# One raw-weight room and two activation rooms in a fused four-layer kernel, with a new instruction order ahead of its tile loop

## The reference, cut to what matters

```python
x = x + tanh(g_xattn[0]) * smoothquant_experts(layernorm(x), fside, ctx)     # layer 1, x is (4, 512, 512)
x = x + tanh(g_ffn[0])   * bit_linear_ffn(layernorm(x), gate_w, val_w, out_w) # layer 2, hidden 2048
x = x + tanh(g_xattn[1]) * (layernorm(x) @ softmax(q @ k.T))                  # layer 3, q, k from ctx
x = x + tanh(g_ffn[1])   * top2_moe(layernorm(x), router_w, down_w, up_w)     # layer 4
# smoothquant linear, per batch b (z=0: x with fside; z=1: silu(gate)*up with ctx)
s  = sqrt(max|x| over rows / max|w| over rows)       # needs column maxima of BOTH operands
xq = round(x/s / row scale); wq = round(w*s / row scale)
y  = xq @ wq.T * scales
```

## Time and profile before

| what | us |
|---|---|
| three timed runs | 467.65, 470.37, 471.56; median 470.37 |
| the profiled execution's own time | 470.85 |
| its span in the trace | 469.1 |
| PE busy in the span | 420.2 (90%) |
| DVE busy | 379.7 (81%) |
| ACT busy | 350.4 (75%) |
| POOL busy | 220.7 (47%) |
| mean granted PE clock | 0.981 of full |

### The profile page before, as it was taken

One profiled execution on the slowest core, in us unless ns is written; L12 is line 12 of the kernel. 1 busy time (PEld: TensorE's weight loads), 2 busy tenths in 40 slices (PEclk: granted clock), 3 DMA queues, 4 the chain that ended last, 5 costly groups with the idle time before them and its releaser, 6 DMA issues.

```text
span 469.1 us, 7365 instructions
## 1 busy us (share of the span) xinstructions
PE 420.2 (90%) x2183; PEld 246.0 (52%) x2183; DVE 379.7 (81%) x955; ACT 350.4 (75%) x574; POOL 220.7 (47%) x343
## 2 busy tenths in 40 slices
PE   4876879977978988689999999999999999999986
PEld 3766647635646434245455545545545554554563
DVE  3889597998893788587898898889889899888853
ACT  1399877796898998857787787778788788777532
POOL 3292684588796744365343333333424333341220
PEclk9987979999999999999999999999999999999999
DMA  8999597354459301511221331231224123122101
GB/s 303 388 386 280 131 340 110 129 168 80 143 131 228 88 7 33 103 30 26 47 47 45 68 59 43 62 75 37 54 68 46 45 67 63 43 67 67 45 25 45
DMA packets 84936, 49.53 MB, mean 106 GB/s; under 512 B 70936, under 2 KB 73496, under 8 KB 83872
## 3 DMA queue, kind: packets, MB, share of 16 engines
q1 hardware_dynamic: 84896, 49.06, 40.3%
HBM read 28.33 MB, written 4.19 MB: 69 GB/s over the span
## 4 chain that ended last, share of the span: by engine, by line
PE 62%; DVE 10%; ACT 9%; DMA 7%; issue 6%; POOL 3%; SPq 2%; ACTq 0%; POOLq 0%; DVEq 0%
PE p_out L1892 11%; PE p_gate L1797 11%; PE p_out L1804 11%; PE p_val L1797 10%; PE p_tr L1779 3%; PE p_out L1826 3%; PE p_out L1852 3%; DMA att_t<-in_L_ffn_gate_w 2%; DMA ctx_sb<-in_ctx 2%; ACT q_room L1282 2%; DMA att_t<-in_L_ffn_out_w 2%; DVE h_max L772 1%; DVE rowmax L812 1%; PE p_val L1748 1%; ACT gate_t L1265 1%
## 5 line engine op out<-in xcount | busy, mean ns | idle before, releaser
L1797 PE MATMUL p_val<-val_t,q_room 128*128 128x512 fp8e4 x256 | 65.7, 379 | 1.4 <-ACT p_val L1407 1.4
L1797 PE MATMUL p_gate<-gate_t,q_room 128*128 128x512 fp8e4 x256 | 65.7, 379 | 0.7 <-DMA q_room<-q_room 0.6
L1804 PE MATMUL p_out<-att_t,qT_room 128*128 128x512 f32 x120 | 55.4, 603 | 1.4 <-ACT qT_room L1227 1.4
L1892 PE MATMUL p_out<-out_t,ws_f 128*128 128x512 fp8e4 x240 | 54.5, 379 | 1.4 <-DMA ws_f<-ws_f 1.4
L594 POOL TENSOR_TENSOR rstd<-mv,ln_eps 128x1 f32<-128x1 f32 x48 | 9.1, 189 | 95.0 <-DVE mv L863 87.9
L1397 ACT ACTIVATE p_gate<-w_slots,seed_scale 128x512 f32<-128x512 f32 x64 | 43.4, 682 | 10.2 <-POOL seed_scale L615 8.9
L892 DVE TENSOR_TENSOR act_f<-p_val,ctx_sb 128x512 f32<-128x512 f32 x64 | 44.1, 689 | 8.4 <-PE p_val L1797 6.1
L1382 ACT ACTIVATE ctx_sb<-p_gate,bcol 128x512 f32<-128x512 f32 x64 | 43.6, 682 | 8.0 <-issue 4.1
L894 DVE TENSOR_REDUCE mu<-act_f 128x1 f32<-128x512 f32 x64 | 43.9, 686 | 2.2
L1407 ACT ACTIVATE p_val<-w_in,seed_scale 128x512 f32<-128x512 f32 x64 | 43.3, 679 | 0.6 <-DVE act_f L892 0.6
L621 POOL TENSOR_TENSOR x_all<-x_all,q_room 128x512 f32<-128x512 f32 x16 | 20.5, 1281 | 45.7 <-ACT q_room L1325 39.1
(11 more groups left out here) (243 smaller groups left out, 989.9 us busy)
## 6 DMA issues: line engine op xcount, KB each, us to landing
att_t<-in_L_ffn_out_w SPq DMA_DIRECT2D x6, 1024.0 KB, 5.0
w_in<-in_fside_BxS2xS SPq DMA_DIRECT2D x4, 1024.0 KB, 7.6
att_t<-in_L_ffn_gate_w SPq DMA_DIRECT2D x4, 1024.0 KB, 13.1
att_t<-in_L_ffn_val_w SPq DMA_DIRECT2D x4, 1024.0 KB, 11.7
out_dram<-x_all SPq DMA_DIRECT2D x15, 256.0 KB, 2.3
x_all<-in_x SPq DMA_DIRECT2D x2, 1024.0 KB, 10.0
x_all<-in_x SPq DMA_DIRECT2D x1, 2048.0 KB, 18.2
ctx_sb<-in_ctx SPq DMA_DIRECT2D x4, 512.0 KB, 5.9
```

The source lines that it names most:

```text
L1797: last = nc.tensor.matmul(bank[:, c % 2, :], x_t[n % 2][:, k * P:(k + 1) * P], w_t[m][:, k, cols], start=False, stop=k == KD - 1, skip_gro ...
L1804: last = nc.tensor.matmul(p_out[:, 0, :], lt_c[:, k * P:(k + 1) * P], att_t[:, bass.ds((n // T) * (KD * S) + k * S, S)], start=k == 0, sto ...
L1892: last = nc.tensor.matmul(p_out[:, 0, :], p_t[:, k * P:(k + 1) * P], w_t[2][:, k, :], start=k == 0, stop=k == KH - 1)
```

## The change

The two buffers of `w_in` become one, and `act_f` becomes two. `fside_load(b)` now waits for `scaled_weights(0, b-1)`; `h_normalise(b)` for the rounding of batch b-2's activations. All five engines get another order ahead of the tiles. No computing instruction is added or removed: the helper calls are the same, each once.

```diff
-        act_f = sb("act_f", [P, T * D], F32)
+        act_f = [sb(f"act_f{r}", [P, T * D], F32) for r in range(2)]
-        w_in = [sb(f"w_in{r}", [P, T * D], F32) for r in range(2)]
+        w_in = sb("w_in", [P, T * D], F32)
-        bias_gate, bias_val = w_slots[...], w_in[0]
-        u = act_f
+        bias_gate, bias_val = w_slots[...], w_in
+        u = act_f[0]
+        def act_of(z, b):
+            return act_f[b % 2] if z == 0 else a_f
         def wt_of(z, b):
-            return w_in[b % 2] if z == 0 else ctx_sb[b % 2]
+            return w_in if z == 0 else ctx_sb[b % 2]
                 def fside_load(b):
-                    need(sp, a_ws[0], b - 1)
+                    need(sp, a_ws[0], b)
                 def val_b_load():
-                    sp.wait_ge(a_ws[0], NB - 1)
+                    sp.wait_ge(a_ws[0], NB)
                 def h_normalise(b):
-                    need(pool, a_q16[0], T * (2 * b - 1))
+                    need(pool, a_q16[0], T * (2 * b - 3))
                 def columns(z, b, r, k):     # PE
-                            pe.wait_ge(fside_loaded[b % 2], 16 * (b // 2 + 1))
+                            pe.wait_ge(fside_loaded, 16 * (b + 1))
```

SP's order, from the x loads on (the calls not shown keep their place):

```diff
+                x_load(2, slice(2, NB))
                 x_load(1, 1)
-                x_load(2, slice(2, NB))
-                fside_load(1)
-                val_load(1)
                 val_load(0)
                 val_load(2)
+                val_load(1)
                 val_load(3)
+                fside_load(1)
                 small_loads()
+                integers(0, 0, 0)
                 integers(0, 0, 1)
-                integers(0, 0, 0)
+                out_load(1)
+                ctx_load(0)
+                ctx_load(1)
                 out_load(0)
                 fside_load(2)
-                ctx_load(0)
-                out_load(1)
-                fside_load(3)
                 integers(0, 1, 0)
                 integers(0, 1, 1)
                 out_load_next(2)
-                ctx_load(1)
+                out_load_next(3)
                 integers(1, 0, 0)
                 integers(1, 0, 1)
-                out_load_next(3)
+                fside_load(3)
                 ctx_load(2)
...
                 integers(1, 1, 0)
+                integers(1, 1, 1)
                 out_load_again(0)
-                val_b_load()
-                integers(1, 1, 1)
-                integers(0, 3, 0)
+                ctx_load(3)
                 out_load_again(1)
+                integers(0, 3, 0)
                 integers(0, 3, 1)
-                ctx_load(3)
+                out_b_load()
                 gate_b_load()
+                val_b_load()
+                x_transpose(0)
                 integers(1, 2, 0)
                 integers(1, 2, 1)
-                x_transpose(0)
                 x_transpose(1)
                 x_transpose(2)
-                out_b_load()
```

More of the change, by code:

```diff
@@ L257, in flamingo_gated_kernel @@
         x_loaded = [sem(f"x_loaded{n}") for n in range(3)]
-        fside_loaded = [sem(f"fside_loaded{r}") for r in range(2)]
+        fside_loaded = sem("fside_loaded")
         ctx_loaded = [sem(f"ctx_loaded{r}") for r in range(2)]
@@ L345, in fside_load @@
                 def fside_load(b):
-                    need(sp, a_ws[0], b - 1)
-                    sp.dma_start(tiles(w_in[b % 2][:, :]), fside[bass.ds(b, 1)].rearrange("b (t p) d -> p (b t) d", p=P)).then_inc(fside_loaded[b % 2], 16)
+                    need(sp, a_ws[0], b)
+                    sp.dma_start(tiles(w_in[:, :]), fside[bass.ds(b, 1)].rearrange("b (t p) d -> p (b t) d", p=P)).then_inc(fside_loaded, 16)
                 def ctx_load(b):
@@ L1068, in _ @@
                 h_scaled_act(1)
-                w_sum(2, 0)
                 h_dequantise(0, 2)
@@ L1085, in _ @@
                 t_reciprocal(0, 0)
-                h_statistics(3)
+                w_sum(2, 0)
                 column_max(0, 2, 0, 0)
@@ L1443, in _ @@
                 w_round(2)
+                w_transposed(0)
                 smooth_rows(0, 0)
-                w_transposed(0)
+                rounded(0, 0, 0)
                 w_transposed(1)
                 w_transposed(2)
+                w_sum(1, 1)
+                w_sum(1, 3)
                 w_transposed(3)
-                rounded(0, 0, 0)
-                w_sum(1, 1)
                 rounded(0, 0, 1)
-                w_sum(1, 3)
                 small_weights()
@@ L1496, in _ @@
                 t_transposed(1, 1)
+                smooth_rows(1, 1)
+                t_exponential(1, 2)
                 rounded(0, 2, 1)
-                t_exponential(1, 2)
                 t_exponential(1, 3)
-                smooth_rows(1, 1)
+                scale_row(0, 2)
                 w_sum(2, 3)
@@ L1563, in _ @@
                 gate_seed(1, 1)
-                q_norm(2)
+                b_gate(1, 0)
+                val_seed(1, 1)
+                q_scaled(2)
+                b_gate(1, 1)
+                gate_seed(1, 2)
+                gate_seed(1, 3)
+                val_seed(1, 2)
+                rounded(1, 3, 0)
+                rounded(1, 3, 1)
+                b_gate(1, 2)
+                silu_loaded()
+                t_transposed(3, 0)
                 t_transposed(3, 1)
                 b_scaled(0, 2)
-                b_gate(1, 0)
-                q_scaled(2)
-                gate_seed(1, 2)
-                b_gate(1, 1)
-                rounded(1, 3, 0)
-                gate_seed(1, 3)
-                rounded(1, 3, 1)
                 b_scaled(0, 3)
-                val_seed(1, 2)
+                scale_row(1, 3)
                 val_seed(1, 3)
-                scale_row(1, 3)
                 t_exponential(3, 2)
                 t_exponential(3, 3)
-                b_gate(1, 2)
+                gate_seed(2, 0)
                 b_gate(1, 3)
+                gate_seed(2, 1)
                 t_transposed(3, 2)
@@ L1921, in _ @@
                 columns(0, 0, 1, 3)
+                clock_raised(2)
                 columns(0, 0, 0, 0)
@@ L1936, in _ @@
                 w_transpose(3)
+                clock_raised(7)
+                clock_raised(6)
+                clock_raised(5)
+                w_total(1)
+                clock_raised(4)
                 columns(0, 1, 1, 0)
+                scale_row(0, 0)
                 columns(0, 1, 1, 1)
                 columns(0, 1, 1, 2)
-                scale_row(0, 0)
-                clock_raised(5)
                 columns(0, 1, 1, 3)
+                small_weights()
                 columns(0, 1, 0, 0)
+                w_transpose(4)
                 columns(0, 1, 0, 1)
-                w_total(1)
                 columns(0, 1, 0, 2)
-                small_weights()
-                w_transpose(4)
                 columns(0, 1, 0, 3)
                 w_transpose(5)
-                clock_raised(4)
                 products(0, 0, 0)
@@ L1997, in _ @@
                 columns(1, 1, 0, 0)
+                columns(1, 1, 0, 1)
+                columns(0, 3, 1, 0)
+                columns(0, 3, 1, 1)
                 t_transpose(1, 0)
                 t_transpose(1, 1)
-                columns(1, 1, 0, 1)
                 t_energies(1, 2)
+                rows(1, 1)
                 t_energies(1, 3)
-                rows(1, 1)
+                scale_row(0, 2)
                 columns(0, 3, 1, 2)
```

294 lines of the change are left out of this document (142 added, 152 removed).

## The result

Over 22 runs each, the kernel after took 468.28 us (median, 466.83 to 472.13) and the kernel before 471.15 (467.65 to 474.01): a ratio of 0.9944, 95% interval 0.9928 to 0.9960. That is 2.9 us or 0.6%, a real gain and a small one. The forecast was 467.4.

The account below looks back on a forecast made before the run. PE bounds the unchanged tile loop, so time won ahead of it passes one for one; DVE, then ACT, bound stretches there. Terms +2.3 - 1.0 - 0.5 - 2.6 - 1.2 = -3.0 us gave 467.4 us, range 462.5 to 474.5.

Parts of the forecast that it names:

- The early part, forecast +2.3: 20 to 56 us: the single raw-weight room makes `smooth(0, 1)` end at 57.9 instead of 55.6, +2.3 us.
- held by fillers and not by the DMA: Before batch 1's columns: `columns(0, 1, 1, 0)` starts at 46 us, behind clock fillers, three of them taking 5.7 us.
- Nothing is lost in bandwidth: Early loads: fside(1) lands at 42 to 43 us, but the val chunks come earlier by as much.
- The second activation room, forecast 0: Early part: it hides nothing that was on the path; taken as 0, its worth between 0 and 1 us.
- 56 to 73, forecast -1.0 and no wait for `w_in`: Batch 0 to 1: 1.0 us regained, `t_query_key(0)` 1.3 later; fside(2) lands at 73.1, 0.8 us before PE wants it.
- The first rival, full clock: Early part and `t_query_key(0)`: clock stays at its upper level, another 4.3 us gained, 463.1 us; chance 0.21.
- 73 to 117, forecast -0.5: DVE's stretch: `h_statistics(3)` leaves, -2.8, and `w_sum(2, 0)` comes in, +2.28; net -0.5 us, standing +0.8.
- 117 to 165, forecast -2.6: ACT's stretch: ready calls fill its idle places and the reload is earlier, -2.0; `scale_row(1, 2)` moves, -0.6 us.
- 165 to 209, forecast -1.2: Path to `b_output(0)`: `smooth_rows(1, 3)` and SP's list release `integers(1, 3, *)` sooner, -1.2 us, bounds 0 and -3.
- tanh, forecast 0: `tanh_gates`, moved to a stretch with Exp's table, needs no table load: 0, with 2.6 us kept for the range.
- The second (raw weights on the path): Late fside(2) landing stops PE at `columns(0, 2, 1, 0)`: +3.3 us in all, 473.7 us; chance 0.24.
- The third (cancel): Whole kernel: early loss and late gain cancel, 470.4 us; chance 0.13.

Follow-up runs that it names:

- run 5: `round_first`: the kernel after with `rounded(0, 3, 0)` ahead of `w_transposed(9)` on ACT; 468.15 us, ratio 0.9950 to the kernel before.
- run 6: The kernel after without the clock fillers `clock_raised` 7, 6, 5 and 4; 467.35 us, ratio 0.9927 to the kernel before.
- run 7: The kernel after with SP issuing `p_transpose(0, 0)` and `(0, 1)` ahead of `integers(1, 3, *)`; 468.04 us, ratio 0.9921 to the kernel before.
- run 8: The kernel after with the changes of run 6 and run 7 joined; 469.16 us, ratio 0.9948 to the kernel before.
- run 9: The kernel after with before's rooms, `h_normalise(2)` and the fside loads placed as those rooms want, loads early; 470.88 us, ratio 0.9999 to before.
- run 10: The kernel after with before's rooms, `h_normalise(2)` behind `h_hidden(0, 3)`, fside(1) behind the value weights; 469.02 us, ratio 0.9945 to before.
- run 12: Run 11 with `h_reciprocal_deviation(2)` ahead of `w_round(4)` and `h_statistics(3)` ahead of `column_max(0, 1, 0, 3)`; 466.76 us, ratio 0.9918 to before.
- run 11: Before's rooms and before's order on all engines up to `smooth(0, 1)`, then the change's order; 474.28 us, ratio 1.0070 to the kernel before.
- run 4: The kernel after with `out_load_again(1)` put back between `integers(0, 3, 0)` and `integers(0, 3, 1)` on SP; 474.45 us, ratio 1.0095 to before.
- the third column: Table column for the profiled execution of run 5, which has the order of the kernel after up to 130 us; span 463.8 us.
- start_fixed: The kernel of run 12: before's start mended, then the change's later order; 466.76 us, ratio 0.9918 to the kernel before.
- run 3: The kernel before with SP's list from `integers(1, 1, 1)` on as in the change, except `x_transpose(0)`; 471.33 us, ratio 0.9995 to before.
- run 1: The kernel before with the change's rooms, only the fside loads and val's bias load moved on SP; 483.86 us, ratio 1.0269 to before.

## Why the prediction came out right, step by step

The total was 0.9 us off, and its sign and size rest on the whole sum; several terms were off in ways that offset each other, and that the sum still came so close is in part luck.

The profiles, one execution of each kernel, can be cut in two at the first context maximum. From there to the end of the span before takes 395.8 us, and the kernel after 393.5. Runs 5, 6, 7, 8, 9, 10 and 12, which have the new order from there on, take 392.5, 392.7, 392.3, 393.2, 393.5, 394.0 and 393.4 (run 11, whose DVE had stood still just ahead of that point, 395.1; run 4, with its stall, 399.0). So the later part is worth 1.8 to 3.5 us, where the forecast had 4.3 (0.5, 2.6 and 1.2). Up to that maximum the same kernels take anything from 69.7 to 76.8 us, against 73.3 before, where the forecast had 1.3 later. The median's -2.9 is thus about what the later part alone gives: its forecast was too large, and the forecast early loss, which would have to be taken off it, isn't seen in the median.

**The early part, forecast +2.3: late, but by something else.** In the profile it is +4.1, in the third column +1.5 (56.97 against 55.46). The start of the columns was right within half a microsecond (46 forecast, 45.52 measured), the landing of fside(1) late by two (42 to 43 forecast, 44.9 measured). The failing step is "held by fillers and not by the DMA": I gave three fillers 5.7 us at the lower clock, and they took 3.41 us, most of it at the upper level (0.78 in the mean from 38 to 40 us, 1.00 from 40 on) and inside a wait (the row at 37.81). `w_total(1)` holds the columns, with the DMA level with it (run 6); that the forecast time was right is luck. I had overlooked that moving `w_total(1)` ahead of the columns ties them to the landing of the last value chunks. "Nothing is lost in bandwidth" says nothing of what PE has waiting for those chunks.

The excess of 1.8 us arose behind that start. From the first column to the last reciprocal the kernel after takes 14.0 us; the forecast had 11.9 to the end of `smooth(0, 1)`. DVE waited 1.16 and 1.87 us for PE (the rows at 46.44 and 49.00), where `scale_row(0, 0)` took 1.92 us at the lower level (the row at 46.19) and stands between the first two columns. In the third column, at the upper level, the same stretch takes 12.85 us (44.12 to 56.97). That price of the clock isn't in the forecast's sum.

**The second activation room, forecast 0.** Right as far as run 10 goes: it puts both rooms back at once, and their sum is nothing measurable. It doesn't show each by itself.

**56 to 73, forecast -1.0 and no wait for `w_in`.** No engine waited for fside(2), issued at 68.73 and landed 6.3 us later. The stretch gave back more, 2.5 us of its 4.1. In the kernel before, `smooth(0, 1)` didn't set the pace here: PE stood for `ctx_load(0)`, which the chain that ended last shows too (first row PE's timeline, second row the chain):

```profile
64.42 1.40 PE L1741 MATMUL p_val<-ident,ctx_sb 128*128 128x128 f32 x8 [2.25 <-DMA ctx_sb<-in_ctx]
```

```profile
55.84 8.54 DMA ctx_sb<-in_ctx
```

In the kernel after it waits for ACT instead (the row at 67.25), 2.8 us later and not 4.1. `t_query_key(0)` then began 2.55 us later, not 1.3, and ran at the lower level again, but for 5.40 us against 6.35. At the upper level it takes 3.70 us: so it ran in the profiles of runs 5, 6 and 7 and of `start_fixed`. In those of runs 8, 9 and 10 it took over 6 us. The first rival, full clock, therefore happens in some executions and not in others; in runs 5 and 7 the order up to this call is that of the kernel after, unchanged. Standing at the end of the stretch: +1.6 measured, +1.3 forecast.

**73 to 117, forecast -0.5.** At `row_scales(0, 2, 0)` the kernel after is 0.45 behind, where I expected 0.8 at the end of the stretch. From the first context maximum to there it gave 1.14 us, in the third column just as much (22.06 us in both, 23.20 before).

**117 to 165, forecast -2.6.** The largest term, and too large. `products(0, 3, 0)` starts at 149.56 against 149.63. So the packing gave 0.5 us from 97 on, not 2.0: ACT is indeed fuller by 0.9 us in the second window, but `rounded(0, 3, 0)` comes 2.7 and `rounded(0, 3, 1)` 5.5 us later than before, as the text had it "against". And ACT isn't what ends this stretch. The chain that ended last goes, in before, from the late reload over POOL to `w_transpose(11)`:

```profile
138.91 7.26 DMA att_t<-in_L_ffn_out_w
...
148.73 1.07 PE p_val L1656 x16
```

In the kernel after it stays on POOL from 124.57 until 145.83, but for gaps of at most 0.6 us each:

```profile
124.57 1.12 POOL w_slots L529
...
129.59 4.93 POOL ws_f L562 x4
...
138.15 2.49 POOL x_all L591 x2
...
144.70 1.13 POOL w_slots L529
145.88 1.07 PE p_val L1659 x16
```

So the change took the reload off the path (run 4 puts it back), and POOL's own list, which the forecast had not looked at, stands there next. That also fits run 5, where another order on ACT moved nothing in the total. No run here changes POOL's list, so this is read from the chain and not tested.

Behind `products(0, 3, 0)` the first `b_chunk` is 1.7 us sooner (164.02), which looks like the forecast's -1.8, and isn't: the change puts it ahead of a 1.03 us product, and at `columns(1, 3, 0, *)` the two kernels are level, 170.72 and 170.85. The reload's mechanism was right; taken out of the new order it costs 6 us (run 4), put into before's order it gains nothing in the total (run 3).

**165 to 209, forecast -1.2.** Measured -0.6. `smooth_rows(1, 3)` is 1.4 us sooner (178.26), but `integers(1, 3, *)` start only 0.3 sooner: `rounded(1, 3, 0)`, at 185.23 against 185.56, now stands behind two gate seeds and a value seed. The wait for `p_transpose` stays, 1.52 us. The cause is as forecast, half of the size is gone.

**tanh, forecast 0.** It runs in 0.20 us at 83.17, between works of Exp and with the next table load only at 87.81. That fits the table sets as the Trainium skill gives them ("ScalarE: Activation LUTs", section "Table sets: the hidden batching unit"). The load itself takes 1.28 us, and the next function starts at 89.11, 1.30 us after the load began. The Trainium skill (same page, section "What ACT_TABLE_LOAD costs") counts 2.66 us with a drain, which this trace doesn't show.

Sum: of the -3.0 forecast, the profiled executions show -0.7 and the medians -2.9. The profile of after fell in a long execution. Against the run with its order up to 130 us and the clock high, the same path is 4.7 us shorter at `c_attend(0)`. So the median's agreement isn't the sum of the profile's terms; what the early terms are worth in a typical execution, between the two columns, stays open to about 2 us. Of the signs named, the loop's period, the missing table load and the missing wait for `w_in` came; `smooth(0, 1)` was 1.6 us later than the 58 named, DVE idle near 70 was 2.25 us and not 3 to 6, and the first loop step 0.51 us sooner and not 3.

**The rivals.** The second (raw weights on the path) didn't come true with the new order: no engine waits for `w_in` in the profile after. With the rooms alone it does, in a kernel 2.7% slower (run 1). The third (cancel) is excluded by the interval. The rooms named in the title give nothing measurable: the order gives the gain, and the single raw-weight room needs that order.

## What to carry to other kernels

When storage and order change together, time the new order with the old storage before crediting the storage: here the new order alone gave the 0.6%, and the rooms nothing that could be measured. A hand-written list for one engine can't be judged or moved alone: one load placed ahead of transposes cost 18 us of queue in one kernel, and was needed in another. A point that comes late is a loss only where it is on the chain: `smooth(0, 1)` was 4.1 us late and the next joint, the first context maximum, 1.6, since before had waited there for a load. And before an engine's list is called the bound, look whether the chain runs over it: from 125 to 146 us it ran over POOL, although ACT was the fuller of the two (19.49 us of 20 against 12.98 from 140 to 160).

## What the runs showed of the hardware

Two executions with the same instructions in the same order up to 130 us stood 2.6 us apart at `smooth(0, 1)` and 3.6 us at the first context maximum. The first part is the landing of the value chunks (`w_total(1)` at 44.34 and 42.93) and the stretch behind it, with the granted clock at 0.50 from 46 to 48 us in the one and 1.00 in the other; the second is `t_query_key(0)`, 5.40 us and 3.70. Which of the two levels an execution gets there isn't set by this order alone. Over the 22 runs of the kernel after the times are over 5 us apart, six times the forecast's error, and a single profile of it can't carry a term ahead of 73 us that is under some 2 us. From the first context maximum to the end the profiles of the new order agree better, 392.3 to 394.0 us.
